# One of sixteen states read out without a transpose, in a fused selective-scan and FFN block

## The chip, the cores and the metric

The kernel runs on one core of one Trainium2 chip. The metric is the device time of one execution in microseconds, as the median of several runs. The engines are TensorE (PE), VectorE (DVE), ScalarE (ACT), Pool (GpSimd) and SyncE (SP), which issues the DMAs.

## The reference, cut to what matters

Input is x of shape (4, 1024, 512). The block adds a layer-normed selective-scan branch to it, and to that a layer-normed FFN branch whose Hadamard transforms the kernel folds into the weights once, at its start. The part that the change touches:

```python
# D_INNER = 1024 channels d, N = 16 states n, A = -exp(a_log)
def step(h, inp):
    dt_t, B_t, C_t, x_t = inp
    dA = jnp.exp(dt_t[..., None] * A)
    h = dA * h + (dt_t * x_t)[..., None] * B_t[:, None, :]
    y = jnp.einsum('bdn,bn->bd', h, C_t)
    return (h, y)
# over the tokens, then
y = y + conv_out * d_param
y = y * jax.nn.silu(gate)
return y @ W_out + b_out
```

So y is a sum over 16 states; each term is the state's h, multiplied by one number of C per token.

## The kernel before, in words

The 4096 tokens go through in 16 chunks of 256. Everything is pipelined over chunks: while chunk c (`cur`) is scanned, chunk c+1 (`front`) gets its projection, convolution and delta, chunk c-1 (`back`) is read out, gated and projected, chunk c-2 (`ff`) goes through the FFN, and chunk c-3 (`fold`) is finished. Each engine has its own program, written out as a function `slot(c, k, ...)` with 32 slots k a chunk, two per state: n = k // 2. Within an engine the order is fixed by that function; between engines there are semaphores only.

The scan keeps channels on partitions: h[n % 2] is a tile of 128 partitions x 8 channel groups x 256 tokens. There are two such tiles, so state n writes over state n-2. For each state:

- ScalarE computes the decays, exp(delta * a), into two PSUM banks, a quarter of the channels at a time (`exps`, L938).
- Pool multiplies u = delta * conv by the row of B, which a DMA has spread over all partitions (`bb`), into dbx (`product`, L1295; `b_times_u`, L1320, once a slot pair). It first copies the last column of state n-2 aside as the carry (`save`, L1278), and it needs the scan of state n-2 to be done.
- VectorE scans, four instructions a state (`scan`, L1112, instruction L1131).
- TensorE transposes h to tokens on partitions, eight 128x128 blocks for each half of the tokens (`turn_h`, L605), into the one PSUM tile hT.
- VectorE adds it to acc with C as its scalar, since C is now one number per partition (`add_h`, L1134, instruction L1144; L1141 for state 0).

After state 15, TensorE transposes acc back in two halves (`turn_y`, L595), VectorE adds conv * D from that PSUM tile in eight instructions (`skip`, L1147, slots 2 and 3 of the next chunk), and Pool multiplies by the gate (`gating`, L1344, slot 6, between the products of states 3 and 4).

Other work that stands in the same slots: TensorE's up_gate (L686) is 24 matmuls into pF. It needs VectorE's `silu_up` (L1161) of two slots earlier, which writes `prod`, to have read pF. silu_up in turn needs ScalarE's `tanh` (L971). ScalarE's `high` (L978) splits prod, and Pool's `low` (L1358, prod_lo) takes the rest. `hidden` (L866) and `down_evac` (L985) empty PSUM banks on ScalarE; `conv_taps` (L888) and Pool's `add_taps` (L1349) make the convolution in slots 8 to 18. `dtin` (L918) holds the transposed delta rows, which TensorE's `dt_proj` (L662) reads in slots 24 to 27. The had matmuls (L740) fold the Hadamard transforms in during chunks 0 and 1.

Of the kernel before, what the change touches and what calls it, by code (L numbers as in the profile page):

```python
# [9 lines left out]
P = 128  # L10
# [7 lines left out]
T = 256  # L18
# [17 lines left out]
def fused_block(nc, x, W, scratch_bc, scratch_ug, scratch_wd, out):  # L36
# [31 lines left out]
    with ctx:  # L68
# [90 lines left out]
        prod_done = sem("prod_done"); dbx_done = sem("dbx_done"); half_done = sem("half_done"); scan_done = sem("scan_done")  # L159
        carry_done = sem("carry_done"); h_turned = sem("h_turned"); acc_done = sem("acc_done")  # L160
        x_turned = sem("x_turned"); xT_evac = sem("xT_evac"); fx_turned = sem("fx_turned"); fx_hi = sem("fx_hi"); fx_lo = sem("fx_lo")
# [10 lines left out]

        SLOTS = 2 * NST
        LAST = NCH + 2
        SPARE = (NCH - 2) * HT
# [11 lines left out]
        for c in range(LAST + 1):  # L187
            cur, front, back, ff = chunk(c), chunk(c + 1), chunk(c - 1), chunk(c - 2)
            if front is not None:
                M_SEQ += [("hid", front, i) for i in range(4)]  # L190
                T_SEQ += [("x", front, 0)]
                PIECES += [("hid", front, dt) for dt in range(DT)]
            if back is not None:
                M_SEQ += [("out", back, i) for i in range(TB)]
                T_SEQ += [("h", back, TB * (NST - 1))]
            if ff is not None:
                T_SEQ += [("f", ff, 0)]
            if back is not None:
                T_SEQ += [("h", back, TB * NST - 1), ("y", back, 0)]
            if cur is not None:  # L200
                M_SEQ += [("gate", cur, i) for i in range(2)]
                PIECES += [("gate", cur, dt) for dt in range(DT)]
                T_SEQ += [("h", cur, 0)]
            if back is not None:
                T_SEQ += [("y", back, 1)]
            if front is not None:
                M_SEQ += [(kind, front, i) for kind, i in M_DELTA]
            if cur is not None:
                M_SEQ += [("gate", cur, i) for i in range(2, 4)]
                T_SEQ += [("h", cur, i) for i in range(1, TB * (NST - 1))]  # L210
        M_NO = {use: i for i, use in enumerate(M_SEQ)}
# [63 lines left out]
        ACT_HID = {2: 0, 4: 1, 6: 2, 8: 3}  # L275
        ACT_TAPS = {8: 0, 9: 1, 10: 2, 12: 3, 13: 4, 14: 5, 15: 6, 16: 7}
        DVE_OUT = {12: 0, 16: 1}
        ACT_GATE = {18: 0, 20: 1, 30: 2}
# [86 lines left out]
        def _(sp):  # L365
# [14 lines left out]
            def free_kept(i):  # L380

                wait_first(sp, y_gated, NCH - 1, sp_passed)
                if i in (1, 2, 3):
                    wait_first(sp, scan_done, NQ * NST * NCH, sp_passed)
                if i in (4, 5):
                    wait_first(sp, h_turned, TB * NST * NCH, sp_passed)

# [37 lines left out]
            def b_rows(j, g):  # L425
                if g < 2:
                    wait_first(sp, bc_stored, 16 * TB * (j + 1), sp_passed)
                if NG * j + g >= 2:

                    wait_first(sp, dbx_done, j * NST + NBG * (g - 1), sp_passed)  # L430
                sp.dma_start(bb[g % 2][:, :, :],
                             scratch_bc[j:j + 1, NBG * g:NBG * (g + 1), :].broadcast_to([P, NBG, T])).then_inc(bb_in[g % 2], 16)

            def load_res(j):
# [39 lines left out]
            def front0():  # L474
# [20 lines left out]
                b_rows(0, 0)  # L495
                b_rows(0, 1)

            def slot(c, k, cur, front, back, ff, fold):
# [14 lines left out]
                if front is not None:  # L513
                    if k == 25:
                        store_bc(front)
                    if k == 27:
                        b_rows(front, 0)
                    if k == 30:
                        b_rows(front, 1)
                for g in HAD_STORE.get((c, k), ()):  # L520
                    store_had(g)
# [24 lines left out]
        def _(pe):  # L546
# [5 lines left out]
            def begin_t(use):  # L552
# [6 lines left out]
                elif kind == "f":  # L559
                    pe.wait_ge(fx_lo, 2 * (j + 1))  # L560
                elif kind == "y":
                    pe.wait_ge(y_skip, DT * j + DT // 2 * (i + 1))
                else:
                    pe.wait_ge(acc_done, NST * TB * j + i + 1)

# [29 lines left out]
            def turn_y(j, i):  # L595
                if i == 0:
                    pe.wait_ge(acc_done, NST * TB * (j + 1))
                begin_t(("y", j, i))
# [150 lines left out]
            def in_slot(c, k, cur, front, back, ff, fold):  # L749
# [21 lines left out]
                if k in (2, 3):  # L771
# [12 lines left out]
                    return  # L784
                if cur is not None:
                    turn_h(cur, n - 1, tb)
# [42 lines left out]
        def _(act):  # L829
# [83 lines left out]
            def turn_rows(j):  # L913
                if j:
                    act.wait_ge(bc_stored, 16 * TB * j)
                full(("turn", j, 0))
                act.activation(bc[:, :], pM[0:TB * 2 * NST, 1, 0:P], ACT.Copy)
                act.activation(dtin[:, :], pM[:, 0, :], ACT.Copy).then_inc(m_evac, 1)  # L918

            def dt_proj(j, pair):  # L920
                full(("dt", j, pair))
                for a in range(2):
                    dt = 2 * pair + a
                    e = act.activation(delta[j % 2][:, dt, :], dt_bank(j, pair)[:, a, :], ACT.Identity if j else ACT.Softplus, bias=b_dt[:, dt:dt + 1])  # L924
                e.then_inc(m_evac, 1)

            def softplus(j):
# [64 lines left out]
            def slot(c, k, cur, front, back, ff, fold):  # L992
# [23 lines left out]
                if front is not None and k in ACT_HID:  # L1016
                    hidden(front, ACT_HID[k])
                if k == 6 and fold is not None:
                    down_evac(fold)
# [57 lines left out]
        def _(dve):  # L1077
# [34 lines left out]
            def scan(c, n, q):  # L1112
# [10 lines left out]
                if q == 0 and NST * c + n >= 2:  # L1123
                    dve.wait_ge(h_turned, TB * (NST * c + n - 1))
                    old, m = divmod(NST * c + n - 2, NST)
                    if saves(old):
                        dve.wait_ge(carry_done, save_no(old, m))
# [6 lines left out]
            def add_h(c, n, tb):  # L1134
                i = NST * TB * c + TB * n + tb
                cn = bcT[c % 2][:, tb, NST + n:NST + n + 1]
# [10 lines left out]
            def skip(j, i):  # L1147
                dve.wait_ge(y_turned, DT // 4 * j + i + 1)
                for a in range(DT // 2):
                    dt = DT // 2 * i + a  # L1150
                    dve.scalar_tensor_tensor(conv[j % 2][:, dt, :], conv[j % 2][:, dt, :], d_skip[:, dt:dt + 1],
                                             hT[:, a * T:(a + 1) * T], ALU.mult, ALU.add).then_inc(y_skip, 1)

# [29 lines left out]
            def in_slot(c, k, cur, front, back, ff, fold):  # L1183
# [20 lines left out]
                if n and cur is not None:  # L1204
                    add_h(cur, n - 1, tb)
                elif n == 0 and back is not None:
                    add_h(back, NST - 1, tb)
# [39 lines left out]
        def _(pool):  # L1247
# [72 lines left out]
            def b_times_u(c, n):  # L1320
# [6 lines left out]
                elif c:  # L1327
                    save(c - 1, NST - 1)
                    pool.wait_ge(scan_done, NQ * NST * c)
                product(c, n, slice(0, DT), dbx_done, prod_no(c, n + 1))  # L1330

# [12 lines left out]
            def gating(j):  # L1344
                pool.wait_ge(y_skip, DT * (j + 1))
                pool.wait_ge(gate_done, j + 1)
# [138 lines left out]
```

## Time and profile before

| | us |
|---|---|
| median of 3 runs (2692.30 to 2695.58) | 2694.03 |
| the profiled execution's own time | 2690.62 |
| its span, first to last instruction | 2688.8 |
| TensorE busy | 2584.6 (96%) |
| VectorE busy | 2239.1 (83%) |
| Pool busy | 2046.8 (76%) |
| ScalarE busy | 1818.1 (68%) |
| mean granted TensorE clock | 0.991 |

A share is an average over the whole span, in which chunks 2 to 14 repeat one pattern and the ends differ. Matmuls are pipelined and their ends are modelled, so starts say more than durations. Idle time of an engine that nobody waits for costs nothing.

### The profile page before, as it was taken

The page shows a single profiled execution, that of the slowest core. Times are in us where ns is not written, and L with a number is a line of the kernel's source. Part 1 is how long each engine was busy: PE and PEld are TensorE (multiplying, and loading weights), DVE is VectorE, ACT ScalarE, POOL GpSimd, SP SyncE. Part 2 cuts the span into 40 slices and gives each one's busy share as a digit, 9 for nine tenths or more (in the row PEclk, how much of TensorE's full clock was granted, in tenths as well). Part 3 has the DMA queues.
Part 4 walks back from the last instruction along what each step waited for, and adds up shares of the span by engine and source line. Part 5 has one row for each costly group of instructions (what it writes and reads, how often), then busy time and mean ns, then how long its engine had stood idle before and what let it go on. Part 6 is the DMA issues. An engine that isn't in the chain of part 4 may idle for free.

```text
span 2688.8 us, 46296 instructions
## 1 busy us (share of the span) xinstructions
PE 2584.6 (96%) x16048; PEld 2191.9 (82%) x16048; DVE 2239.1 (83%) x2567; ACT 1818.1 (68%) x3939; POOL 2046.8 (76%) x1692
## 2 busy tenths in 40 slices
PE   7899889999999999999999999999999999989987
PEld 5566568989888888988888888988888888878786
DVE  6698799898889889898889889898889888889321
ACT  4576677777777777777777777777777777755221
POOL 6576779788797979888797979888797979766222
PEclk9999999999999999999999999999999999999999
DMA  5554245766666665766666665766666665656564
GB/s 179 192 187 155 104 160 200 235 208 228 220 222 222 218 221 199 240 212 225 220 225 224 215 221 201 236 210 231 220 226 217 220 214 200 216 188 227 227 258 173
DMA packets 165193, 564.41 MB, mean 210 GB/s; under 512 B 17248, under 2 KB 19680, under 8 KB 132960
## 3 DMA queue, kind: packets, MB, share of 16 engines
q1 hardware_dynamic: 164960, 561.44, 60.5%
q8 instruction: 129, 2.11, 0.3%
q14 instruction: 104, 0.85, 0.1%
HBM read 527.30 MB, written 34.08 MB: 209 GB/s over the span
## 4 chain that ended last, share of the span: by engine, by line
PE 77%; DVE 10%; ACT 7%; issue 3%; DMA 2%; POOL 1%; SPq 0%; POOLq 0%; DVEq 0%; ACTq 0%
PE pF L703 21%; PE hT L610 13%; PE pM L628 13%; PE pD L719 10%; PE pM L680 8%; DVE h L1131 5%; DVE acc L1144 3%; PE pD L740 3%; PE pM L650 3%; PE decay L703 2%; PE hT L602 1%; ACT decay L952 1%; PE pF L740 1%; ACT delta L929 1%; ACT delta L924 1%
## 5 line engine op out<-in xcount | busy, mean ns | idle before, releaser
L1131 DVE TENSOR_TENSOR_SCAN h<-decay,dbx 128x512 f32<-128x512 f32 x1024 | 1201.2, 1206 | 97.6 <-ACT decay L952 68.1
L1299 POOL TENSOR_TENSOR dbx<-u,bb 128x2048 f32<-128x2048 f32 (+1 forms) x272 | 1179.1, 4335 | 37.7 <-DVE h L1131 35.7
L952 ACT ACTIVATE decay<-delta,a_neg 128x255 f32<-128x255 f32 x2048 | 875.5, 468 | 309.4 <-DVE h L1131 302.3
L703 PE MATMUL pF<-fxT_hi,wug 128*128 128x256 f32 x3744 | 735.2, 289 | 6.6 <-DMA wug<-scratch_ug 4.5
L1144 DVE SCALAR_TENSOR_TENSOR acc<-hT,bcT,acc 128x1024 f32<-128x1024 f32 x480 | 609.7, 1270 | 126.8 <-PE hT L610 123.4
L703 PEld LDWEIGHTS pF<-fxT_hi,wug 128*128 128x128 f32 x3744 | 604.1, 193 | 8.3 <-DMA wug<-scratch_ug 5.8
L610 PEld LDWEIGHTS hT<-ident,h 128*128 128x128 f32 x4096 | 472.3, 141 | 150.0 <-issue 96.9
L610 PE MATMUL hT<-ident,h 128*128 128x128 f32 x4096 | 534.6, 274 | 34.9 <-DVE acc L1144 22.5
L703 PE MATMUL pF<-fxT_lo,wug 128*128 128x256 f32 x1872 | 531.9, 284 | 0.0
L628 PE MATMUL pM<-xnT,w_in 128*128 128x256 f32 x2016 | 480.5, 381 | 10.6 <-ACT hid L872 4.9
L628 PEld LDWEIGHTS pM<-xnT,w_in 128*128 128x128 f32 x2016 | 366.2, 191 | 56.2 <-ACT hid L872 6.5
L1363 POOL TENSOR_TENSOR prod_lo<-prod,prod_hi 128x256 fp32r<-128x256 f32 x256 | 187.2, 731 | 293.0 <-ACT prod_hi L983 292.3
L703 PEld LDWEIGHTS pF<-fxT_lo,wug 128*128 128x128 f32 x1872 | 361.8, 193 | 0.2
L719 PE MATMUL pD<-wd,prod_hi 128*128 128x512 f32 x976 | 351.6, 441 | 3.8 <-POOL prod_lo L1363 2.0
L1356 POOL TENSOR_TENSOR conv<-conv,tap 128x256 f32<-128x256 f32 x360 | 261.3, 731 | 30.8 <-ACT tap L898 12.0
L680 PE MATMUL pM<-w_out,gate 128*128 128x512 f32 x512 | 240.4, 593 | 4.3 <-ACT hid L872 2.3
L719 PEld LDWEIGHTS pD<-wd,prod_hi 128*128 128x128 f32 x976 | 177.1, 190 | 59.6 <-issue 30.0
L719 PE MATMUL pD<-wd,prod_lo 128*128 128x512 f32 x488 | 192.8, 395 | 0.0
L976 ACT ACTIVATE th<-pF,half_gate 128x256 f32<-128x256 f32 x240 | 111.9, 466 | 107.1 <-PE pF L703 104.9
L898 ACT ACTIVATE tap<-hid,taps 128x256 f32<-128x256 f32 x360 | 155.6, 497 | 0.0
L1285 POOL COPY carry<-h 128x8 f32<-128x8 f32 x192 | 36.9, 192 | 149.3 <-issue 96.2
L1166 DVE SCALAR_TENSOR_TENSOR prod<-th,pF 128x256 f32<-128x256 f32 x240 | 98.7, 411 | 58.5 <-ACT th L976 58.5
(170 smaller groups left out, 2711.5 us busy)
## 6 DMA issues: line engine op xcount, KB each, us to landing
wug<-scratch_ug SPq DMA_DIRECT2D x244, 1024.0 KB, 4.8
wd<-scratch_wd SPq DMA_DIRECT2D x244, 512.0 KB, 4.0
w_in<-in_W_in SPq DMA_DIRECT2D x252, 256.0 KB, 2.9
bb<-scratch_bc SPq DMA_DIRECT2D x128, 256.0 KB, 4.7
xb<-in_hidden_states SPq DMA_DIRECT2D x16, 512.0 KB, 4.8
xr<-in_hidden_states SPq DMA_DIRECT2D x16, 512.0 KB, 6.0
out<-xr SPq DMA_DIRECT2D x16, 512.0 KB, 3.7
kept_ug<-scratch_ug SPq DMA_DIRECT2D x6, 1024.0 KB, 9.1
```

What stands on the lines that cost most here:

```text
L610: mm = pe.transpose(hT[:, dt * P:(dt + 1) * P], h[n % 2][:, dt, tb * P:(tb + 1) * P], ident[:, :])
L628: mm = pe.matmul(pM[:, a, :], w[:, kt, :], xnT[j % 2][:, kt, :], start=(kt == 0), stop=(kt == KT - 1))
L680: mm = pe.matmul(o, gate[:, dt, tb * P:(tb + 1) * P], w_out[:, dt, :], start=(dt == 0), stop=(dt == DT - 1))
L703: mm = pe.matmul(gate_up_bank(no)[:, which, :], ug_tile(no)[:, 2 * which + a, kt, :], fxT[b][:, kt, :], start=(kt == 0 and i == 0), stop=( ...
L719: mm = pe.matmul(pD[tb][:, :], split[a][:, tb * P:(tb + 1) * P], wd_tile(no)[:, b, :], start=(ft == 0 and i == 0), stop=(ft == HT - 1 and ...
L898: e = act.activation(tap[dt % 2][:, k, :], hid[:, dt, k:k + T], ACT.Copy, scale=taps[:, dt, k:k + 1])
L952: e = act.activation(da[q % 2][:, i, 1:], delta[c % 2][:, dt, 1:], ACT.Exp, scale=a_neg[:, dt, n:n + 1])
L1131: dve.tensor_tensor_scan(row(h[n % 2][:, tiles, :]), row(da[q % 2][:, :, :]), row(dbx[n % 2][:, tiles, :]), 0.0, ALU.mult, ALU.add).then_i ...
L1144: dve.scalar_tensor_tensor(acc[c % 2][:, tb, :], hT[:, :], cn, acc[c % 2][:, tb, :], ALU.mult, ALU.add).then_inc(acc_done, 1)
L1299: pool.tensor_tensor(dbx[n % 2][:, tiles, :], u[:, tiles, :], rows, ALU.mult).then_inc(done if restarts(c) else prod_done, 1)
L1356: pool.tensor_tensor(conv[j % 2][:, dt, :], conv[j % 2][:, dt, :], tap[dt % 2][:, k, :], ALU.add).then_inc(tap_added, 1)
L1363: pool.tensor_tensor(prod_lo[no % 2][:, :], prod[no % 2][:, :], prod_hi[no % 2][:, :].bitcast(F32), ALU.subtract).then_inc(p_lo, 1)
```

## The change

State 2 of each chunk (`DIRECT = 2`, the third) is no longer transposed. Pool multiplies its h by the row of C in place, in the scan's layout. The row comes by a DMA that spreads it over all partitions, into `dtin`, once `dt_proj` has read that tile. VectorE adds the result to conv, in one instruction of 128x2048 in slot 7. For that ScalarE multiplies conv by D beforehand, in place, in slots 4 to 6, when u has been made from it. `skip` then only adds acc's transposed halves, in two instructions. The semaphore counts follow: h_turned and acc_done count 15 states a chunk.

```diff
+        DIRECT = 2
+        NTURN = NST - 1
+        def turn_no(j, n, tb):
+            return TB * (NTURN * j + n - (n > DIRECT)) + tb
...
-                T_SEQ += [("h", cur, i) for i in range(1, TB * (NST - 1))]
+                T_SEQ += [("h", cur, i) for i in range(1, TB * (NST - 1)) if i // TB != DIRECT]
...
+        ACT_SKIP = {4: range(0, 3), 5: range(3, 6), 6: range(6, 8)}
...
+            def load_c(j):                                             # SP
+                wait_first(sp, m_filled, M_NO["dt", j, 3] + 1, sp_passed)
+                wait_first(sp, bc_stored, 16 * TB * (j + 1), sp_passed)
+                sp.dma_start(dtin[:, :].rearrange("p (a t) -> p a t", a=1),
+                             scratch_bc[j:j + 1, NST + DIRECT:NST + DIRECT + 1, :].broadcast_to([P, 1, T])).then_inc(c_in, 16)
...
                 b_rows(0, 1)
+                load_c(0)
...
+                    if k == 31:
+                        load_c(front)
...
-                if cur is not None:                                    # PE
+                if cur is not None and n - 1 != DIRECT:
                     turn_h(cur, n - 1, tb)
...
+                    act.wait_ge(direct_done, j)                        # ACT, turn_rows
...
+            def scale_skip(j, tiles):
+                if 0 in tiles:
+                    act.wait_ge(u_done, 2 * (j + 1))
+                for dt in tiles:
+                    e = act.activation(conv[j % 2][:, dt, :], conv[j % 2][:, dt, :], ACT.Copy, scale=d_skip[:, dt:dt + 1])
+                if DT - 1 in tiles:
+                    e.then_inc(skip_scaled, 1)
...
                     hidden(front, ACT_HID[k])
+                if cur is not None and k in ACT_SKIP:
+                    scale_skip(cur, ACT_SKIP[k])
...
-                    dve.wait_ge(h_turned, TB * (NST * c + n - 1))      # DVE, scan
                     old, m = divmod(NST * c + n - 2, NST)
+                    if m == DIRECT:
+                        dve.wait_ge(direct_added, old + 1)
+                    else:
+                        dve.wait_ge(h_turned, turn_no(old, m, TB - 1) + 1)
...
             def skip(j, i):
-                dve.wait_ge(y_turned, DT // 4 * j + i + 1)
-                for a in range(DT // 2):
-                    dt = DT // 2 * i + a
-                    dve.scalar_tensor_tensor(conv[j % 2][:, dt, :], conv[j % 2][:, dt, :], d_skip[:, dt:dt + 1],
-                                             hT[:, a * T:(a + 1) * T], ALU.mult, ALU.add).then_inc(y_skip, 1)
+                dve.wait_ge(y_turned, 2 * j + i + 1)
+                dve.wait_ge(direct_added, j + 1)
+                half_tiles = conv[j % 2][:, DT // 2 * i:DT // 2 * (i + 1), :].rearrange("p d t -> p (d t)")
+                dve.tensor_tensor(half_tiles, half_tiles, hT[:, :], ALU.add).then_inc(y_skip, 1)
+            def add_direct(c):
+                dve.wait_ge(skip_scaled, c + 1)
+                dve.wait_ge(direct_done, c + 1)
+                flat = lambda t: t[:, :, :].rearrange("p d t -> p (d t)")
+                dve.tensor_tensor(flat(conv[c % 2]), flat(conv[c % 2]), flat(h[DIRECT % 2]), ALU.add).then_inc(direct_added, 1)
...
                 if n and cur is not None:
-                    add_h(cur, n - 1, tb)
+                    if n - 1 != DIRECT:
+                        add_h(cur, n - 1, tb)
+                    elif tb:
+                        add_direct(cur)
...
+                if n == DIRECT + 2:                                    # Pool, b_times_u
+                    pool.wait_ge(c_in, 16 * (c + 1))
+                    if saves(c):
+                        pool.wait_ge(carry_done, save_no(c, DIRECT))
+                    pool.tensor_tensor(h[DIRECT % 2][:, :, :], h[DIRECT % 2][:, :, :],
+                                       dtin[:, :].rearrange("p (a t) -> p a t", a=1).broadcast_to([P, DT, T]), ALU.mult).then_inc(direct_done, 1)
                 product(c, n, slice(0, DT), dbx_done, prod_no(c, n + 1))
```

## Rows read from the trace of the kernel before

**Rows 1.** The page's part 4: the chain that ended last, by engine.
```profile
PE 77%; DVE 10%; ACT 7%; issue 3%; DMA 2%; POOL 1%; SPq 0%; POOLq 0%; DVEq 0%; ACTq 0%
```
**Rows 2.** Stages, one steady chunk: stretch, its us, busy us (instructions), clock, DMA share, GB/s.
```profile
1315.00:1466.00 151.00, 150.17 (x981) 131.56 (x980) 135.21 (x157) 111.84 (x243) 125.75 (x104) 1.00 0.64 220
```
**Rows 3.** The chain in order of time, slots 8 and 9: start, us, what.
```profile
1329.45 0.87 PE hT L610 x8
1330.33 2.88 PE pF L703 x24
...
1334.07 0.87 PE hT L610 x8
```
**Rows 4.** Groups by line and form, whole span: busy us, mean ns, idle before.
```profile
L1299 POOL TENSOR_TENSOR dbx<-u,bb 128x2048 f32<-128x2048 f32 x240 | 1102.9, 4595 | 36.1 <-DVE h L1131 35.7 <-issue 0.4
L1144 DVE SCALAR_TENSOR_TENSOR acc<-hT,bcT,acc 128x1024 f32<-128x1024 f32 x480 | 609.7, 1270 | 126.8 <-PE hT L610 123.4
...
L895 ACT ACTIVATE conv<-hid,b_conv,taps 128x256 f32<-128x256 f32 x120 | 71.5, 596 | 39.4 <-POOL conv L1356 38.8
...
L1151 DVE SCALAR_TENSOR_TENSOR conv<-conv,d_skip,hT 128x256 f32<-128x256 f32 x128 | 52.7, 474 | 8.4 <-PE hT L602 7.6
```
**Rows 5.** Timeline of the setup, VectorE and Pool: start, us, instruction, idle before.
```profile
23.23 3.49 DVE L341 TENSOR_TENSOR had_pong<-had_pong,had_wscale 128x3200 f32<-128x3200 f32 x1 [14.12 <-DMA had_pong<-in_W_down]
...
44.90 5.37 DVE L341 TENSOR_TENSOR had_pong<-had_pong,had_wscale 128x3200 f32<-128x3200 f32 x1
...
23.28 5.39 POOL L341 TENSOR_TENSOR had_pong<-had_pong,had_wscale 128x896 f32<-128x896 f32 x1 [15.68 <-DMA had_pong<-in_W_down]
...
43.25 3.67 POOL L341 TENSOR_TENSOR had_pong<-had_pong,had_wscale 128x896 f32<-128x896 f32 x1
```
**Rows 6.** Timeline of Pool, slots 6 to 8 of the steady chunk.
```profile
1314.53 0.73 POOL L1363 TENSOR_TENSOR prod_lo<-prod,prod_hi 128x256 fp32r<-128x256 f32 x1 [0.96 <-ACT prod_hi L983]
1315.22 4.57 POOL L1347 TENSOR_TENSOR gate<-conv,gate 128x2048 f32<-128x2048 f32 x1
...
1319.87 4.62 POOL L1299 TENSOR_TENSOR dbx<-u,bb 128x2048 f32<-128x2048 f32 x1
```
**Rows 7.** Timeline of ScalarE, slots 4 to 9.
```profile
1310.74 0.81 ACT L872 ACTIVATE hid<-pM,b_in 128x256 f32<-128x256 f32 x2
...
1314.05 0.40 ACT L983 ACTIVATE prod_hi<-prod 128x256 fp32r<-128x256 f32 x1
...
1320.02 1.09 ACT L990 ACTIVATE fo<-pD 128x512 f32<-128x512 f32 x2 [0.55 <-PE pD L719]
...
1329.33 1.30 ACT L898 ACTIVATE tap<-hid,taps 128x256 f32<-128x256 f32 x3
```
**Rows 8.** Timeline of VectorE, end of slot 7 and start of slot 8.
```profile
1327.46 0.42 DVE L1168 TENSOR_TENSOR prod<-pF,prod 128x256 f32<-128x256 f32 x1
1327.80 2.33 DVE L1131 TENSOR_TENSOR_SCAN h<-decay,dbx 128x512 f32<-128x512 f32 x2
```
**Rows 9.** Timeline of Pool in chunk 0.
```profile
106.63 0.19 POOL L1285 COPY carry<-h 128x8 f32<-128x8 f32 x1 [6.54 <-issue]
```
**Rows 10.** The chain in order of time, chunk 1.
```profile
263.15 10.39 DMA scratch_ug<-had_r_hi
...
276.22 1.72 PE pD L740 x4
```
**Rows 11.** Chunk 15: timeline of Pool, and the chain in order of time.
```profile
2374.20 4.59 POOL L1347 TENSOR_TENSOR gate<-conv,gate 128x2048 f32<-128x2048 f32 x1
...
2387.65 3.90 PE pF L703 x24
```
**Rows 12.** Timeline of Pool and VectorE, the product of state 10 and its scan.
```profile
1377.78 4.60 POOL L1299 TENSOR_TENSOR dbx<-u,bb 128x2048 f32<-128x2048 f32 x1
...
1385.95 2.33 DVE L1131 TENSOR_TENSOR_SCAN h<-decay,dbx 128x512 f32<-128x512 f32 x2
```
**Rows 13.** The page's part 6: queue, count, KB each, us to landing.
```profile
bb<-scratch_bc SPq DMA_DIRECT2D x128, 256.0 KB, 4.7
```

More of the change, by code:

```diff
@@ L159, in fused_block @@
         prod_done = sem("prod_done"); dbx_done = sem("dbx_done"); half_done = sem("half_done"); scan_done = sem("scan_done")
-        carry_done = sem("carry_done"); h_turned = sem("h_turned"); acc_done = sem("acc_done")
+        carry_done = sem("carry_done"); c_in = sem("c_in"); skip_scaled = sem("skip_scaled"); direct_done = sem("direct_done"); direct_added = sem("direct_added"); h_turned = sem("h_turned"); acc_done = sem("acc_done")
         x_turned = sem("x_turned"); xT_evac = sem("xT_evac"); fx_turned = sem("fx_turned"); fx_hi = sem("fx_hi"); fx_lo = sem("fx_lo")
@@ L385, in free_kept @@
                 if i in (4, 5):
-                    wait_first(sp, h_turned, TB * NST * NCH, sp_passed)
+                    wait_first(sp, h_turned, TB * NTURN * NCH, sp_passed)
             def load_ug(j, ft):
@@ L561, in begin_t @@
                 elif kind == "y":
-                    pe.wait_ge(y_skip, DT * j + DT // 2 * (i + 1))
+                    pe.wait_ge(y_skip, 2 * j + i + 1)
                 else:
-                    pe.wait_ge(acc_done, NST * TB * j + i + 1)
+                    pe.wait_ge(acc_done, turn_no(j, *divmod(i, TB)) + 1)
             def piece(kind, j, dt):
@@ L596, in turn_y @@
                 if i == 0:
-                    pe.wait_ge(acc_done, NST * TB * (j + 1))
+                    pe.wait_ge(acc_done, NTURN * TB * (j + 1))
                 begin_t(("y", j, i))
@@ L1134, in add_h @@
             def add_h(c, n, tb):
-                i = NST * TB * c + TB * n + tb
+                i = turn_no(c, n, tb)
                 cn = bcT[c % 2][:, tb, NST + n:NST + n + 1]
@@ L1344, in gating @@
             def gating(j):
-                pool.wait_ge(y_skip, DT * (j + 1))
+                pool.wait_ge(y_skip, 2 * (j + 1))
                 pool.wait_ge(gate_done, j + 1)
```

## The prediction

> **What bounds the kernel now.** I read the page's chain of waits first [rows 1]: TensorE makes 77% of it, VectorE 10%, ScalarE 7%, Pool 1%. Then one steady chunk by stages [rows 2]: 151.0 us, with TensorE busy for 150.2 of them, VectorE 135.2, Pool 125.8, ScalarE 111.8. So a chunk costs TensorE's work, and the other three matter only where TensorE reaches a semaphore before them. Whether such a place arises has to be read slot by slot around the changed state, and I did that on the chunk whose slots 4 to 9 lie at 1310 to 1335 us.
>
> A name for what follows: T0 = 1330.33 us, where up_gate of slot 8 starts (the pF row of [rows 3]). Before it TensorE runs without a gap. It needs the product written by silu_up of slot 7, done at 1327.88 [rows 8], which is 2.45 us early.
>
> **Removed from TensorE.** Slots 6 and 7 lose eight transposes each. The chain gives 0.87 us for eight [rows 3], so 1.74 us a chunk, 28 us over 16 chunks. Without a new wait TensorE would be at up_gate of slot 8 at 1330.33 - 1.74 = 1328.6.
>
> **VectorE's sum is about even.** Two adds of 1.27 us go, and eight skip operations (52.7 us in all, 3.3 a chunk, since in a run they overlap) [rows 4]. In their place come two of 128x1024 from PSUM, nearest to the 1.27 us of an add, and one of 128x2048. For the latter the setup has the right kind: 3200 elements in 3.49 us with nobody ahead of it [rows 5], 1.09 us per thousand, so 2.3 us for 2048. Net -0.9 us a chunk. The skip saving I cost at nothing: in slots 2 and 3 VectorE waits for TensorE's transposes right after it, and below nothing it could not go by more than 0.7 us. The even sum hides the matter, which is where the 128x2048 addition stands and what it needs.
>
> **The addition and Pool need the same thing.** It has two inputs in SBUF. No VectorE operation of the steady chunks has: scan, add, skip and silu_up each read one operand from PSUM. The setup shows what happens when such an operation meets a Pool operation [rows 5]. Started together, VectorE's took 3.49 us and Pool's 896 elements 5.39; the second time Pool's was there first (43.25 to 46.92), and VectorE's same 3200 elements took 5.37, until 50.27: from 46.92 that is 3.35, its own time. They run one after the other, whole instruction by whole instruction. In the steady state Pool's operations are 4.6 us long [rows 4].
>
> The Trainium skill, page "SBUF — State Buffer", section "Who interferes with whom", says the same of a VectorE instruction with two SBUF inputs and a Pool instruction that reads SBUF: whoever starts first keeps the shared port pair for the whole instruction. By that rule the chunk comes out as forecast below; without it, as in the second rival. The setup rows agree with it at 3200 elements against 896; no row of the steady state tests it.
>
> **Pool.** It gets a 128x2048 product, 4.6 us like its others. It goes between the gating and the product for state 4, and Pool has no room there [rows 6]: prod_lo ends at 1315.3, gating follows at once to 1319.8, the carry copy to 1319.9, state 4's product to 1324.5. VectorE takes that product at 1327.80 [rows 8], so the cover is 3.3 us and the insert is 4.6. Before it come a wait for the carry copy (0.15, from the spacing of such a copy and the next product) and a later start: ScalarE scales three tiles in slot 4, ahead of the exponentials and prod_hi of slot 5. Three copies with a scale take 1.30 us [rows 7]; hid ends at 1311.55, so the exponentials go from 1312.85 to 1314.5 and prod_hi starts 0.45 us later than its 1314.05. Then direct runs 1320.5 to 1325.1, and state 4's product 1325.1 to 1329.7.
>
> **ScalarE otherwise.** The three tiles of slot 5 shift that slot's tanh by 1.7 us, to about 1316.6, and VectorE reads it at 1317.7: hidden. The two of slot 6 (0.87 us) push the pD evacuation from 1320.02 to about 1320.3: hidden but for 0.3 us, since it sets when the exponentials of slot 7 start. If that cover were gone the shift would be at most 1.3 us once a chunk.
>
> **VectorE in slot 7.** The add of slot 6 is gone, but the scan of slot 7 waits for its exponentials, as now. So scan, statistics, scan end near 1326.0 as before, not two microseconds earlier. VectorE then takes the addition. Direct is done (1325.1), but Pool is already inside state 4's product, until 1329.7. So: blocked 3.7 us, 2.3 us of its own to 1332.0, silu_up 0.85 (two instructions like the one in [rows 8]) to 1332.85, and up_gate can start at about 1333.1 with the 0.2 us such hand-overs take. Against T0 that is **+2.8 us a chunk**: a 4.5 us stall less the 1.74 saved. Were VectorE to win the port, Pool's product would end at 1325.1 + 2.3 + 4.6 = 1332.0, two scans (2.33) and an add (1.28) would follow to 1335.7, and TensorE's transposes of slot 9, at 1334.07 now, would come 1.6 us late. The bounds for one chunk are thus +1.6 and +2.8; I take the upper since Pool goes from one product to the next in its own queue while VectorE is still in its scan.
>
> **After it.** Relative to the shifted up_gate, VectorE runs some 2 us behind and has it back within three states (it waits for TensorE's transposes ahead of its adds for 123.4 us in all, 7.7 a chunk [rows 4]). Pool's queue is 2.2 us later relative to TensorE (prod_lo of slot 8 and the product of state 5 queue behind the blocked addition). Pool has almost no idle time between the product of state 6 and that of state 10, so I look at the last: it ends at 1382.4 and is taken at 1385.95 [rows 12]. Of those 3.5 us 1.3 are left, so no further loss.
>
> **C's row.** One DMA a chunk, half the bytes of a bb load (4.7 us to landing [rows 13]), issued in slot 31 and used in slot 8 of the next chunk, some 35 us on: nothing. On SP's queue it stands behind a wait for the dt products of slot 27, passed by then; in front0 it may hold the queue for up to 2 us once. Its own issue is about 0.3 us on a queue that waits for TensorE.
>
> **The odd chunks.** Chunk 0 has no gating, and Pool idles for several microseconds ahead of each product [rows 9]: the saving stays, -1.7. Chunk 1: up to 273.5 the chain is in a 10.39 us DMA wait [rows 10], nothing. Chunk 15, at a lower clock: gating ends 2378.8, so direct to 2383.8 (0.45 included), product to 2388.4, addition 2390.7, silu_up 2391.6, up_gate at 2391.7 against 2387.65: +4.0 [rows 11].
>
> **Sum.** Chunks 2 to 14: 13 x 2.8 = 36.4; chunk 15 +4.0; chunk 0 -1.7: +38.7. The profiled execution took 2690.6 us for its span of 2688.8, so 2729.3; the median of the runs is 3.4 above it, so **2733 us**.
>
> **Rivals.**
> 1. *Pool's lateness is not absorbed.* ScalarE's taps wait for Pool's additions of taps (38.8 us in all [rows 4]), and exponentials stand behind them. If the 2.2 us comes through once a chunk: +2.2 x 13 = 29, 2762. For it: that wait is there already. Against: TensorE's next needs have 1.3 to 2 us of slack by my count.
> 2. *Faster: the two engines do not exclude each other in the steady state.* Then the addition runs 1326.0 to 1328.3 beside Pool's product, up_gate starts about 1329.3, and state 4's product at 1329.7 decides: scans to 1332.0, add to 1333.3, transposes of slot 9 at 1333.5 against 1334.07. That is -0.55 x 14 - 1.7 = -9.5, so 2684. It decides as soon as the addition takes under about 3 us in place. Against: the setup rows, in which every meeting is serial.
> 3. *The plain count.* Both Pool's insert and the addition are hidden and the 28 us of transposes come off whole: 2666. It needs 1.3 us more room on Pool than [rows 6] show.
> 4. *The clock.* A 4.5 us stall lets TensorE's clock fall. After the 10.39 us DMA wait the had matmuls ran at their old 1.72 us for four [rows 10], so one stall does not do it. If each chunk lost 5 us more: about 2800.
> 5. *VectorE wins the port*: 13 x 1.6 + 2 = +23, 2717.
>
> **How the numbers follow.** Forecast 0.52, rival 1 0.13, rival 5 0.12, rival 4 0.04, rival 2 0.12, rival 3 0.03, and 0.04 for gain and loss that cancel within 0.2% (5.4 us, what a measurement of this kernel can tell). Faster 0.15, same 0.04, slower 0.81. The range 2698 to 2765 leaves out rivals 2 to 4 and the cancelling case, near enough two in ten.
>
> **What would show it.** Right: the VectorE addition averages 5 to 6 us, not 2.3; TensorE waits about 4.5 us a chunk at pF (L703) for VectorE's prod; ScalarE's new scaling costs no TensorE wait; the chunk is near 153.8 us; transposes fall by 256. Wrong: an addition of 2.3 us beside Pool's product, or a chunk of 150.5 us.

## The result, and the profile after

The changed kernel takes 2746.06 us (median of 4, 2744.82 to 2748.20) against 2693.47 for the kernel before: ratio 1.0201, interval 1.0187 to 1.0215. That is 52.6 us slower; forecast were 2733 us and +38.7.

The page of the kernel after, chain and costliest changes. Its parts answer to [rows 1, 4]: TensorE has gone from 77% of the chain to 70%, VectorE from 10% to 14%, and the line of up_gate's matmuls now carries a wait for VectorE's prod.

```profile
span 2746.4 us, 45876 instructions
...
PE 2588.5 (94%) x15792; PEld 2193.1 (80%) x15792; DVE 2270.3 (83%) x2455; ACT 1863.2 (68%) x4067; POOL 2148.2 (78%) x1708
...
PE 70%; DVE 14%; ACT 9%; issue 5%; DMA 2%; POOL 1%; SPq 0%; POOLq 0%; DVEq 0%; ACTq 0%
...
L721 PE MATMUL pF<-fxT_hi,wug 128*128 128x256 f32 x3744 | 756.6, 295 | 61.4 <-DVE prod L1205 56.4
```

Groups by line and form of the kernel after: the addition, Pool's product with C, ScalarE's scaling, the new skip (busy us, mean ns, idle before).

```profile
L1189 DVE TENSOR_TENSOR conv<-conv,h 128x2048 f32<-128x2048 f32 x16 | 85.0, 5315 | 1.4 <-POOL h L1374 1.4
L1374 POOL TENSOR_TENSOR h<-h,dtin 128x2048 f32<-128x2048 f32 x16 | 73.4, 4588 | 2.1 <-POOL carry L1325 2.1
L950 ACT ACTIVATE conv<-conv,d_skip 128x256 f32<-128x256 f32 x128 | 56.0, 500 | 0.0
L1183 DVE TENSOR_TENSOR conv<-conv,hT 128x1024 f32<-128x1024 f32 x32 | 38.8, 1211 | 7.9 <-PE hT L620 7.0
```

The same chunk as in [rows 3, 6 and 8], in the timelines of Pool and then VectorE. Its slots 6 to 8 now lie at 1341 to 1358 us.

```profile
1341.20 4.57 POOL L1393 TENSOR_TENSOR gate<-conv,gate 128x2048 f32<-128x2048 f32 x1
1345.71 0.20 POOL L1325 COPY carry<-h 128x8 f32<-128x8 f32 x1
1346.09 4.59 POOL L1374 TENSOR_TENSOR h<-h,dtin 128x2048 f32<-128x2048 f32 x1 [0.17 <-POOL carry L1325]
1350.64 4.55 POOL L1339 TENSOR_TENSOR dbx<-u,bb 128x2048 f32<-128x2048 f32 x1
1355.16 2.77 POOL L1409 TENSOR_TENSOR prod_lo<-prod,prod_hi 128x256 fp32r<-128x256 f32 x1
```

```profile
1350.46 1.19 DVE L1163 TENSOR_TENSOR_SCAN h<-decay,dbx 128x512 f32<-128x512 f32 x1
1351.57 5.78 DVE L1189 TENSOR_TENSOR conv<-conv,h 128x2048 f32<-128x2048 f32 x1
1357.27 0.41 DVE L1203 SCALAR_TENSOR_TENSOR prod<-th,pF 128x256 f32<-128x256 f32 x1
1357.71 0.42 DVE L1205 TENSOR_TENSOR prod<-pF,prod 128x256 f32<-128x256 f32 x1
```

The addition starts 0.93 us after Pool's product for state 4 and cannot get going until that ends at 1355.19; 2.16 us later it is done. Then it is Pool's turn: prod_lo takes 2.77 us instead of 0.73. And silu_up is queued behind the addition. The chain in order of time shows what TensorE makes of it: up_gate of slot 8 starts at 1358.28, and its 24 matmuls take 5.46 us where [rows 3] has 2.88.

```profile
1337.17 2.88 PE pF L721 x24
...
1351.57 5.78 DVE conv L1189
1357.35 0.34 DVE prod L1203
1357.69 0.02 issue
1357.71 0.44 DVE prod L1205
1358.15 0.14 issue
1358.28 5.46 PE pF L721 x24
1363.74 0.86 PE pM L698 x2
```

The stages around it (columns as in [rows 2]) give the reason for the 5.46 us. TensorE is idle from about 1354.3 on. The granted clock is 1.00 up to 1354, 0.83 on the mean of the idle stretch, and 0.50 to 0.52, the lower level (1.2 GHz), while up_gate runs.

```profile
1350.00:1354.00 4.00, 4.00 (x23) 3.46 (x22) 3.94 (x5) 2.35 (x7) 4.00 (x2) 1.00 0.79 268
1354.00:1358.20 4.20, 0.35 (x4) 0.10 (x1) 4.17 (x4) 1.01 (x3) 4.20 (x4) 0.83 0.75 270
1358.20:1361.00 2.80, 2.72 (x13) 2.75 (x14) 2.80 (x3) 1.46 (x4) 2.80 (x1) 0.50 0.02 6
1361.00:1363.70 2.70, 2.70 (x14) 2.70 (x14) 2.70 (x3) 2.32 (x6) 2.53 (x4) 0.52 0.00 0
1363.70:1370.00 6.30, 6.30 (x30) 4.03 (x29) 4.53 (x8) 6.04 (x13) 5.87 (x8) 1.00 0.60 208
```

Measured by the starts of Pool's gating, which comes once a chunk, a steady chunk takes 155.10 us (411.66 to 2427.91 over 13) against 151.05 (410.58 to 2374.20 over 13): +4.05 each. Below, "a chunk" is always this measure.

### The profile page after: what moved, and what is told of

The parts are those of the page before. It is cut to its first block, busy times and chain, and to the rows that moved or that the text cites. A ratio compares the mean times of both kernels' runs of the same rounds, so it can differ in the third digit from the quotient of the medians.

```text
span 2746.4 us, 45876 instructions
## 1 busy us (share of the span) xinstructions
PE 2588.5 (94%) x15792; PEld 2193.1 (80%) x15792; DVE 2270.3 (83%) x2455; ACT 1863.2 (68%) x4067; POOL 2148.2 (78%) x1708
## 3 DMA queue, kind: packets, MB, share of 16 engines
q1 hardware_dynamic: 167264, 563.54, 59.1%
q8 instruction: 127, 2.08, 0.3%
## 4 chain that ended last, share of the span: by engine, by line
PE 70%; DVE 14%; ACT 9%; issue 5%; DMA 2%; POOL 1%; SPq 0%; POOLq 0%; DVEq 0%; ACTq 0%
PE pF L721 20%; PE hT L628 12%; PE pM L646 11%; PE pD L737 8%; PE pM L698 8%; DVE h L1163 6%; DVE acc L1176 3%; PE pD L758 3%; DVE conv L1189 3%; PE pM L668 3%; PE decay L721 2%; ACT decay L979 2%; PE hT L620 1%; PE pF L758 1%; ACT delta L956 1%
## 5 line engine op out<-in xcount | busy, mean ns | idle before, releaser
L721 PE MATMUL pF<-fxT_hi,wug 128*128 128x256 f32 x3744 | 756.6, 295 | 61.4 <-DVE prod L1205 56.4
L721 PEld LDWEIGHTS pF<-fxT_hi,wug 128*128 128x128 f32 x3744 | 623.3, 199 | 67.3 <-issue 62.5
L1176 DVE SCALAR_TENSOR_TENSOR acc<-hT,bcT,acc 128x1024 f32<-128x1024 f32 x448 | 568.3, 1269 | 119.6 <-PE hT L628 116.7
L628 PEld LDWEIGHTS hT<-ident,h 128*128 128x128 f32 x3840 | 442.6, 141 | 141.7 <-issue 92.3
L721 PE MATMUL pF<-fxT_lo,wug 128*128 128x256 f32 x1872 | 543.0, 290 | 0.0
L628 PE MATMUL hT<-ident,h 128*128 128x128 f32 x3840 | 501.2, 274 | 30.9 <-DVE acc L1176 19.0
L1409 POOL TENSOR_TENSOR prod_lo<-prod,prod_hi 128x256 fp32r<-128x256 f32 x256 | 193.2, 755 | 268.3 <-ACT prod_hi L1010 267.7
L721 PEld LDWEIGHTS pF<-fxT_lo,wug 128*128 128x128 f32 x1872 | 373.5, 200 | 0.8
L698 PEld LDWEIGHTS pM<-w_out,gate 128*128 128x128 f32 x512 | 89.3, 193 | 68.7 <-issue 63.1
```

The lines of the kernel that those rows point to most:

```text
L628: mm = pe.transpose(hT[:, dt * P:(dt + 1) * P], h[n % 2][:, dt, tb * P:(tb + 1) * P], ident[:, :])
L698: mm = pe.matmul(o, gate[:, dt, tb * P:(tb + 1) * P], w_out[:, dt, :], start=(dt == 0), stop=(dt == DT - 1))
L721: mm = pe.matmul(gate_up_bank(no)[:, which, :], ug_tile(no)[:, 2 * which + a, kt, :], fxT[b][:, kt, :], start=(kt == 0 and i == 0), stop=( ...
L1176: dve.scalar_tensor_tensor(acc[c % 2][:, tb, :], hT[:, :], cn, acc[c % 2][:, tb, :], ALU.mult, ALU.add).then_inc(acc_done, 1)
L1409: pool.tensor_tensor(prod_lo[no % 2][:, :], prod[no % 2][:, :], prod_hi[no % 2][:, :].bitcast(F32), ALU.subtract).then_inc(p_lo, 1)
```

## The experiments

All edits are against the changed kernel; ratios are against the kernel before, which was measured again beside each group of experiments (medians 2691.20 us for 1 to 4, 2690.75 for 5 to 8, 2690.03 for 9 to 11). The changed kernel was measured once, beside 2693.47, so a difference in us between it and an experiment is good to some 3 us.

**1. The addition with one input in PSUM.** From chunk 2 on:

```diff
-                dve.tensor_tensor(flat(conv[c % 2]), flat(conv[c % 2]), flat(h[DIRECT % 2]), ALU.add)
+                dve.wait_ge(tanh_done, (c - 2) * HT + 3)
+                dve.tensor_tensor(four, four, two, ALU.add)    # two = pF, broadcast to 4 x 512
```

> From chunk 2 on, the addition in slot 7 reads pF (PSUM), broadcast to 2048 elements, in place of the state, after a wait for that slot's tanh; so it has one SBUF input, and state 2's term is left out of y. Pool's product of the state with C stays, and so does the lateness of the product for state 4. Theory (the addition is blocked by Pool's running product, 3.6 us of its 5.8): the addition takes 2.3 us, TensorE waits about 0.5 us for prod in slot 8 and 0.5 us in slot 9, its clock does not fall, and the total is 2680 to 2692 us. Rival (Pool's insert is the loss, the product for state 4 comes too late whatever the addition does): TensorE waits 3 us or more in slot 9 instead, 2725 or more. Rival (VectorE's larger load in slot 7): the addition is as long as before, about 2746.

2693.14 us, ratio 1.0006 (0.9997 to 1.0015); a chunk 151.28. The top of the expectation is missed by a microsecond, and the verdict is clear: at the same place, with Pool's queue as full, the addition takes 2.26 us, and 53 us are gone. In no steady chunk does the clock fall behind the addition. Its timeline, VectorE:

```profile
1328.95 2.26 DVE L1195 TENSOR_TENSOR conv<-conv,pF 128x2048 f32<-128x2048 f32 x1
...
1332.62 2.34 DVE L1163 TENSOR_TENSOR_SCAN h<-decay,dbx 128x512 f32<-128x512 f32 x2 [0.62 <-POOL dbx L1345]
```

Pool's product for state 4 ran from 1328.0 to 1332.6 beside it. The 0.62 us, which the scan waits for Pool, is what is left of Pool's insert once the addition is not held up: the 3.3 us by which [rows 6] show the product to be early are used up, and a little more.

**2. No product with C on Pool.** The addition has its two SBUF inputs.

```diff
-                if n == DIRECT + 2:
-                    pool.wait_ge(c_in, 16 * (c + 1))
...
-                    pool.tensor_tensor(h[DIRECT % 2][:, :, :], h[DIRECT % 2][:, :, :], ..., ALU.mult).then_inc(direct_done, 1)
```

> Pool does not multiply state 2 by C; the addition adds the bare state, with both inputs in SBUF as in the changed kernel. Left out: the factor C of that term. Theory: the product for state 4 ends before the addition starts, so that what is left on the port is short; the addition takes 2.3 to 3 us, TensorE's wait in slot 8 is 0.6 to 1.2 us, no fall of the clock, total 2676 to 2688 us. Should Pool's product of state 5 get the port first, the addition takes 5.5 us or more and the total stays near 2740. Rival (it is the addition's two SBUF inputs, whatever Pool's queue holds): 2740.

2673.33 us, 0.9934 (0.9918 to 0.9950); a chunk 149.89. A little below the expected range. Pool in this kernel: the carry copy, 0.19 us elsewhere, starts 0.24 us after the addition (1319.56 to 1321.83) and ends as it does. VectorE was first here.

```profile
1319.80 2.08 POOL L1325 COPY carry<-h 128x8 f32<-128x8 f32 x1 [0.65 <-issue]
1321.84 4.61 POOL L1339 TENSOR_TENSOR dbx<-u,bb 128x2048 f32<-128x2048 f32 x1
```

**3. TensorE kept busy in its wait.**

```diff
+                    if k == 8 and ff is not None:       # same waits, then four more times
+                        for again in range(4):
+                            for dt in range(DT):
+                                pe.transpose(hT[:, dt * P:(dt + 1) * P], h[(n - 1) % 2][:, dt, 0:P], ident[:, :])
                     turn_h(cur, n - 1, tb)
```

> The changed kernel with the eight transposes of slot 8 done five times over instead of once from chunk 2 on, writing the same values (3.5 us of TensorE work that lies inside its wait for prod). Theory (the fall of the granted clock after that wait costs 2 to 2.6 us a chunk): up_gate after it takes 2.88 us for 24 matmuls instead of 5.46, the total falls by 25 to 35 us, to 2711 to 2721. Rival (the clock falls for another reason, or the loss is made good elsewhere): 2740 to 2750. If the added work does not fit into the wait: above 2750.

2726.51 us, 1.0127 (1.0112 to 1.0143); a chunk 153.61. The mechanism is right, the size was too high: up_gate takes 3.11 us, the granted clock of the span is back from 0.979 to 0.991 (that of the kernel before), and 19.6 us are won, not 25 to 35. I had taken the 5.46 us of one chunk for all; over the 13 steady chunks of the changed kernel up_gate takes 4.39 to 5.46 us, 4.89 on the mean. The chain of this kernel:

```profile
1340.96 5.77 DVE conv L1195
...
1347.68 3.11 PE pF L721 x24
```

The addition is blocked as before (5.77 us), so of the 52.6 us some 20 are the clock and 33 the rest, the delay above all.

**4. VectorE first.**

```diff
+                    pool.wait_ge(direct_added, c + 1)
                 product(c, n, slice(0, DT), dbx_done, prod_no(c, n + 1))
```

> The changed kernel with Pool waiting for the addition before it starts the product for state 4, so that VectorE has the port. Theory (Pool's insert and the port in series, whichever is first): addition 2.3 us, TensorE's wait in slot 8 falls to 0.6 us and one of 3.5 us appears in slot 9, where transposes wait for the add behind the scans of state 4; at that point +2.2 us a chunk against the kernel before instead of +4.7; total 2720 to 2735, at the upper end if the clock falls after the new wait too. Rival (order alone is the fault): below 2700.

2749.84 us, 1.0219 (1.0202 to 1.0236); a chunk 155.33. The addition takes 2.27 us in all 16 chunks, both inputs in SBUF, so it was Pool's product that made it longer and not what it reads. The wait went where it was expected: TensorE's waits for prod fall to 9.4 us in all, those of its transposes for the adds rise from 19.0 to 71.2. The total is above the range because I had added up badly: +2.2 and 2.4 for the clock, the upper end that I meant, make 4.6 x 13 = 60, not 45. The clock falls after the new wait in 10 of the 13 steady chunks. In the chunk whose gating starts at 1344.53 eight transposes then take 1.97 us instead of 0.87 and six matmuls 3.02 instead of 2.58. Pool idles 3.24 us for VectorE, which is still in its scan when the product with C ends.

```profile
PE hT L628 <- DVE acc L1176: 71.2, 43, 3.7
...
PE pF L721 <- DVE prod L1205: 9.4, 15, 2.0
```

**5. Nothing in place of state 2.** No transposes, product, scaling or addition for it; skip without D.

```diff
-                dve.tensor_tensor(flat(conv[c % 2]), flat(conv[c % 2]), flat(h[DIRECT % 2]), ALU.add).then_inc(direct_added, 1)
-                if cur is not None and k in ACT_SKIP:
-                    scale_skip(cur, ACT_SKIP[k])
...          # and Pool's product, as in 2
```

> State 2 and D's product are left out of y altogether: no transposes of that state, no product with C, no scaling by ScalarE, no addition. It measures what the removed transposes and adds are worth when nothing takes their place. Plain count: 16 x 1.74 = 28 us, 2661 to 2669 us. Rival (another engine is next at once): 2675 or more. Theory for the comparison with the kernel that only lacks Pool's product (2673): the addition and the scaling beside it cost 0 to 12 us.

2661.05 us, 0.9888 (0.9871 to 0.9904); a chunk 149.28, 1.77 less than before. The plain count of 1.74 is what the transposes are worth. Experiment 2 is 12 us slower, at the top of the expected 0 to 12: that is the addition, the scaling and what else 5 leaves out.

**6. No scaling by D.**

```diff
-                if cur is not None and k in ACT_SKIP:
-                    scale_skip(cur, ACT_SKIP[k])
```

> The changed kernel without ScalarE's scaling by D in slots 4 to 6 (y has conv, not conv times D). The scaling stands in the chain of the changed kernel twice: prod_hi of slot 5 0.45 us late, and the exponentials of slot 7 0.8 us late. Theory (the stall ends when Pool's product for state 4 does, so only what delays Pool counts): 0.3 to 0.5 us a chunk, 2738 to 2743. Rival (the delay of VectorE's scan counts): 1 us a chunk or more, 2733 or less.

2746.81 us, 1.0203 (1.0183 to 1.0224). The four runs spread over 9.5 us, so the median alone could not tell the expected 5 us; but a chunk takes 155.08 us against 155.10, and even the 0.4 us a chunk is missing. The scaling stands in the chain of the changed kernel without costing anything that shows: TensorE's wait for prod is 56.4 us with it and without it.

**7. State 10 instead of state 2.**

```diff
-        DIRECT = 2
+        DIRECT = 10
```

> The changed kernel with state 10 read out directly instead of state 2 (same product, same addition, same scaling; Pool's product in slot 24, ahead of that of state 12, the addition in slot 23). In the kernel before, Pool's product for state 12 ends 6.5 us before it is taken, against 3.3 for state 4, and VectorE waits 1.3 us for TensorE where the addition goes. Theory (place decides: no cover at state 4, cover at state 12): the addition is blocked about 1.5 us instead of 3.6, no fall of the clock, total 2680 to 2705. Rival (the method costs that much anywhere): above 2730.

2731.22 us, 1.0149 (1.0132 to 1.0166): a miss. The cover on Pool was there, but VectorE, rid of the add of slot 22, came to the addition 1.6 us after Pool's product had started, not near its end, and silu_up was again behind it. TensorE's wait for prod (38.4 us in all) was again followed by a fall of the clock, in 12 of the 13 steady chunks: up_gate then took 4.38 to 4.61 us. Neither was expected. Pool, then VectorE:

```profile
1420.83 4.60 POOL L1339 TENSOR_TENSOR dbx<-u,bb 128x2048 f32<-128x2048 f32 x1
```

```profile
1422.39 5.19 DVE L1189 TENSOR_TENSOR conv<-conv,h 128x2048 f32<-128x2048 f32 x1
1427.50 0.41 DVE L1203 SCALAR_TENSOR_TENSOR prod<-th,pF 128x256 f32<-128x256 f32 x1
```

**8. State 0, D's product on VectorE.**

```diff
-        DIRECT = 2
+        DIRECT = 0
+                if k == 3 and cur is not None:      # ahead of the last scan of state 1
+                    add_direct(cur)
...
+                for dt in range(DT):
+                    e = dve.scalar_tensor_tensor(conv[c % 2][:, dt, :], conv[c % 2][:, dt, :], d_skip[:, dt:dt + 1],
+                                                 h[DIRECT % 2][:, dt, :], ALU.mult, ALU.add)
```

> State 0 is read out directly. Pool idles 2.3 and 3.8 us in slots 4 to 6 of the kernel before, so its product goes ahead of that of state 2, where 4 us or more are free; VectorE adds in slot 3, before its last scan of state 1, for which Pool has to wait anyway, so nothing of Pool holds the port. D's product is made by VectorE in that addition, in eight instructions (3.5 to 4 us), not by ScalarE; C's row is loaded in slot 28. Theory (cover on Pool and a free port are all that was lacking): no instruction of the addition is blocked, TensorE's wait for prod stays under 1 us a chunk, total 2665 to 2685, faster than the kernel before. Rival (VectorE is late at slot 4, since eight instructions take the place of one add): 2690 to 2710.

2736.71 us, 1.0165 (1.0146 to 1.0184), at a span's clock of 0.980: the worst miss. The eight instructions met the last 0.9 us of Pool's product and took 4.50 us. But what counts is that they stand before a scan: TensorE's transposes of state 1 wait for it, 60.8 us in all, up to 6.2 each. That wait is in neither expectation; I had looked at the port and at prod only.

```profile
PE hT L627 <- DVE h L1158: 60.8, 15, 6.2
```

**9. silu_up ahead of the addition.**

```diff
-                    elif tb:
-                        add_direct(cur)
...
                 if k >= 3 and k % 2 and ff is not None:
                     silu_up(ff, (k - 3) // 2)
+                if tb and cur is not None and n - 1 == DIRECT:
+                    add_direct(cur)
```

> The changed kernel with VectorE's silu_up of slot 7 ahead of the addition instead of behind it; nothing else. The addition is as blocked as before. Theory (the wait for prod is silu_up's place behind a blocked instruction; behind it stands a second wait, scans of state 4 and the add that frees hT): TensorE's wait for prod goes, and one of about 3 us for hT comes in slot 9; +1.2 us a chunk against the kernel before, and up to 2.4 more where the clock falls; 2710 to 2735. Rival (silu_up's place is all of the loss): below 2690. Rival (the order of the two changes nothing): 2746.

2726.72 us, 1.0134 (1.0119 to 1.0149). The wait for prod no longer appears; transposes wait for the adds, 61.3 us in all against 19.0, and the span's clock is 0.983. The place of silu_up's two instructions is worth 19 us, and the next wait stands close behind.

```profile
PE hT L628 <- DVE acc L1176: 61.3, 43, 4.9
```

**10. State 10 with silu_up ahead**: edits 7 and 9 together.

> State 10 read out directly, with silu_up of slot 23 ahead of the addition. With state 10 the product for state 12 was in time (no wait of the scan), but VectorE came to the addition 1.5 us after that product had started and was blocked 3 us, with silu_up behind it. Theory (that is why the kernel with state 10 missed its 2680 to 2705): the wait for prod (38 us in all there) goes, the next need, hT in slot 25, is met about when it is in the kernel before; 2685 to 2705. Rival (VectorE is the bound in slots 24 to 29, and its lateness costs the same): 2720 or more.

2708.85 us, 1.0064 (1.0049 to 1.0079); 4 us above the range. A chunk takes 151.74. Against experiment 7 that is 22 us less, so silu_up's place, with the fall of the clock that followed from it, was the larger part of its miss: here the clock does not fall behind the addition in any steady chunk. The addition now averages 2.98 us; transposes waiting for adds (57.2 us) are what remains.

**11. The other half of the change alone.** All states transposed; scaling on ScalarE and the two-instruction skip stay.

```diff
-        DIRECT = 2
-        NTURN = NST - 1
+        DIRECT = 99
+        NTURN = NST
```

> Only the other half of the change: ScalarE scales conv by D in slots 4 to 6 and VectorE's skip is two instructions; all sixteen states are transposed as in the kernel before, and there is no product with C and no addition. Theory (this half is hidden): within 0.3% of the kernel before, 2685 to 2700. Rival (ScalarE's scaling in slot 6 makes the scans of slot 7 late and costs about 0.8 us a chunk): 2703 or more.

2688.47 us, 0.9991 (0.9981 to 1.0000): no difference that this kernel's measurement tells. The loss is all in the way that state 2 takes.

All by the same measure of a chunk:

| kernel | us | a chunk against before |
|---|---|---|
| changed | 2746.1 | +4.0 |
| no scaling (6) | 2746.8 | +4.0 |
| VectorE first (4) | 2749.8 | +4.3 |
| TensorE kept busy (3) | 2726.5 | +2.6 |
| silu_up first (9) | 2726.7 | +2.8 |
| addition not held up, Pool's insert kept (1) | 2693.1 | +0.2 |
| insert gone, addition kept (2) | 2673.3 | -1.2 |
| nothing in its place (5) | 2661.1 | -1.8 |

## Why the prediction was right, and where its size was off

- *TensorE saves 1.74 us a chunk.* Shown: 1.77 in experiment 5.
- *VectorE's operations.* New skip 1.21 us (taken 1.27), addition 2.27 us unblocked (taken 2.3), Pool's product 4.59 (4.6). Right. (My terms for VectorE's sum add up to -1.0, not -0.9; nothing rests on it.)
- *Pool has no room ahead of state 4's product.* Shown by experiment 1: with the addition not held up, the insert alone spends the whole saving, and a chunk is 0.2 us longer than before. My second rival had -0.55 a chunk for that case and 2684 us, against 2693 measured: TensorE's waits for prod and hT were longer than I had them.
- *The addition is blocked until that product ends.* Right to half a microsecond: forecast 3.7 + 2.3 us, measured 3.6 + 2.2 in the chunk shown; the 16 additions average 5.3 us in all. Experiment 1, which takes only the second SBUF input away, is worth 53 us, and experiment 2 shows the mirror image, a Pool copy held for 2.08 us. From up_gate of slot 4 (1311.38 us before, 1337.17 after) to that of slot 8 it is 18.95 us before and 21.11 after: +2.2 against the +2.8 forecast. TensorE's wait for prod is 56.4 us over 15, 3.8 each, not 4.5.
- *The clock* is the term that was mis-sized, and its evidence was misread. I put its fall at nothing in the sum and gave it 0.04, because after a 10.39 us DMA wait the matmuls kept their 1.72 us [rows 10]. But that wait is the chain's, not TensorE's: TensorE is busy for 8.97 of those 10.39 us, and its own wait before the matmuls is 2.34 us (first two rows below). In the changed kernel its wait at that place is 3.19 us, and the matmuls take 3.02. The trace of before also held the opposite case, 40 us further on: after a wait of 1.98 us four such matmuls take 2.92. In the changed kernel the clock falls once in each of the 13 steady chunks, after the wait for prod (3.4 to 4.7 us). Over those chunks up_gate takes 2.0 us more on the mean; the chunk shown, with 2.58, is one of the five longest. Experiment 3 prices it at 19.6 us in all. Without it the changed kernel is at 2726.5, beside a forecast of 2733.
- *Some luck.* The two errors pull against each other: the delay was put at +2.8 us a chunk and is 2.0 (a wait of 3.75 on the mean, less 1.74), the clock was put at nothing and adds 2.0. Together that is the +4.05 of a chunk, and it is why the total is still inside the range, though a rival that the range was meant to leave out came true in part: rival 4 had 5 us a chunk and about 2800.
- *Rival 1*, Pool's lateness coming through in the taps, costs TensorE nothing that shows. ScalarE's wait for Pool's additions of taps does rise, from 38.8 to 59.1 us in all, but no wait of that kind appears among TensorE's, and the +4.05 of a chunk leaves no room for 2.2 more. In the chunk shown slot 8 is 2.2 + 2.6 = 4.7 us late, and the next gating comes 4.5 us late (155.51 us after the last, against 150.99).
- *Rival 5*, VectorE getting the port first, was priced at 2717; forced in experiment 4 it cost 2750. I had left out that Pool must then wait for VectorE's scan, and the clock: my sum let the addition start at 1325.1, though by my own rows VectorE is free at 1326.0.
- *ScalarE's scaling is hidden.* Right, and more so than I had it: of the 0.45 us I let it add to Pool's start nothing is to be seen. Pool's prod_lo of slot 5 starts 3.34 us after up_gate of slot 4 with the scaling and without it (experiment 6).
- *The odd chunks.* The first gating comes 2.2 us sooner (253.87 against 256.03), forecast 1.7. That does not show the saving: experiment 11, which transposes every state, has it at 253.45. Chunk 1 was put at nothing; the next gating is 1.1 us late, so chunk 1 cost 3.2 in this execution, part of it the slower matmuls after TensorE's wait; the rest is open. From slot 6's gating to up_gate of slot 8, chunk 15 takes 16.7 us against 13.45 [rows 11]: +3.3 against +4.0.

The rows for the clock: the stretch of the DMA in [rows 10] (columns as in [rows 2]), then two of TensorE's waits in the kernel before and the four matmuls after the second, then up_gate of slot 8 in two other chunks of the changed kernel.

```profile
263.15:273.54 10.39, 8.97 (x41) 6.24 (x40) 8.47 (x8) 3.94 (x10) 7.15 (x5) 1.00 0.94 319
...
275.09 1.12 PE L680 MATMUL pM<-w_out,gate 128*128 128x512 f32 x2 [2.34 <-ACT hid L872]
...
314.05 1.62 PE L628 MATMUL pM<-xnT,w_in 128*128 128x256 f32 x4 [1.98 <-DVE ob L1104]
...
315.67 2.92 PE pD L740 x4
```

```profile
1668.48 5.46 PE pF L721 x24
...
1978.51 4.39 PE pF L721 x24
```

The Trainium skill, page "SBUF — State Buffer", section "Who interferes with whom", says that outside the two-port modes a VectorE instruction contends with Pool only if it has two SBUF inputs, and that whichever starts first keeps the shared pair to its end. Both halves agree with the runs: the PSUM form ran its 2.26 us beside Pool's product, and in each meeting shown the later one ended only after the other had (the copy of experiment 2 with it).

## What to carry to other kernels

Before moving work to Pool and its result to VectorE, list what each holds at that moment: a VectorE instruction with two SBUF inputs, placed where Pool goes from one long product to the next, costs Pool's remaining time on top of its own. Everything queued behind such an instruction pays as well, so put what another engine waits for ahead of it. And price a new wait of TensorE with the slower clock after it, unless several instances in the trace say otherwise; take as an instance only a wait of TensorE itself, since a long wait in the chain can be one through which TensorE works on.

## What the runs showed of the hardware that I had not expected

- A TensorE wait of 3.9 us in otherwise full work was followed by 24 matmuls in 5.46 us instead of 2.88, at a granted clock of 0.50 to 0.52. The length of a wait does not settle it alone: in the kernel before, TensorE waits of 1.97 and 1.98 us, 20 us apart, were followed by four like matmuls in 1.72 and in 2.92 us, and in experiment 4 the new wait was 3.72 us in ten of the 13 steady chunks, and in one of these ten the clock stayed at 1.00.
- Small Pool instructions suffer as the large ones do: a 128x8 copy took 2.08 us instead of 0.19, a prod_lo 2.77 instead of 0.73.
- 3.5 us of useless transposes in a wait made the kernel 19.6 us faster.
